# Two layers of a hybrid model on one core: where the two expert slots are added up

## The chip, the core and the metric

The kernel runs on one core of a Trainium2 chip. The metric is the device time of one execution in microseconds; the median of three runs of the kernel before is 1312.31 us (1311.45 to 1312.48). Shorter is better.

## The reference

The model takes x of shape (4, 256, 256) in float32, four sequences of 256 tokens with 256 features, and adds eight stages to it, each on a layer-normed copy. Stage 2 and stage 4 are the same expert stage, which the change touches; stage 3 is an attention over the 16 heads within a token. The others are two causal attentions, a gated delta rule and two dense feed-forward stages. The expert stage, shortened:

```
logits = x @ Wg.T                      # 8 experts
probs = softmax(logits)
rw, sel = top_k(probs, 2)
rw = rw / rw.sum(-1)                   # two gates per token
base1, base3 = x @ W1.T, x @ W3.T      # shared, F = 896
for k in range(2):                     # the two slots
    x1 = base1 + lora(A1, B1, sel[k])  # rank 32 per expert
    x3 = base3 + lora(A3, B3, sel[k])
    x2 = silu(x1) * x3                 # 896 per token
    down = x2 @ W2.T                   # shared weights
    a2 = (x2 @ A2.T)[sel[k]]           # 8 x 32, one expert's 32 kept
    out += (down + a2 @ B2[sel[k]]) * rw[k]
```

## The kernel before, in words

Everything stays in SBUF; weights are loaded once. A sequence is worked on alone, as two halves of 128 tokens, but the order of the work is written out by hand in `program` (line 423) so that stages of different sequences stand beside each other. Each engine runs the same `program` and executes its own table entry of each stage name, so the queue of every engine (TensorE, VectorE, ScalarE as ACT, GpSimd as POOL) follows the one written order. PSUM banks are handed out by a small planner, `Ring`, which takes the bank of the permitted lane that was claimed the longest ago.

An expert block is (k, s): layer part k (0 or 1) and sequence s (0 to 3), eight blocks. `experts` (line 590) loops over seven feature tiles m of 128 (F = 896) with a lag of two:

- `x_first` (k, (s, m)): eight 256-column float32 matmuls give x1 and x3 of tile m for slot 0 in one bank. ACT applies Silu (line 1329), VectorE multiplies (line 1725) into `x2T[s][:, 0, m]` and signals `x2_first`.
- `x_second`: four matmuls add to the same bank the difference between the adapters of slot 1 and slot 0; ACT and VectorE again, into `x2T[s][:, 1, m]`; the signal is the drain of the bank.
- `down` (line 909): for slot i and token half a, seven matmuls with `x2T[s][:, i, m]` as stationary operand and 512 moving columns, which are 256 of the shared down weights W2 and 256 of A2 for all experts. In four of the blocks (`weave`) slot 0's part is spread over the loop instead, as `down_sum` (line 922). VectorE then adds the first 256 columns times the gate to X (line 1740) and keeps the chosen expert's 32 of the other 256, times the gate (line 1744, with `onehotw`, built in `gates`, line 1690).
- `lora_t` and `lora` bring the adapters' second half.

`middle` (line 501) runs twice, for sequences (0, 1) and (2, 3). It weaves the block (0, b) with the attention within tokens (`token_heads`, line 570) of sequence a, and the block (1, a) with that of sequence b, where a is the first and b the second of the pair. That attention's products are 16 GpSimd operations of 128x1024 for a sequence (`head_prod`, line 2138), each reduced on VectorE (lines 1785 and 1803); a buffer holds four of them. At the end `head_out_t` transposes the result on TensorE, inside the down group of slot 1 (place "down10": behind the first token half). GpSimd has otherwise only the powers of the norms (line 2116) and some work of the delta rule. The block (0, a) has no head products beside it; neither has (1, b).

Of the kernel before, what the change touches and what calls it, by code (L numbers as in the profile page):

```python
# [12 lines left out]
P = 128  # L13
B, T, D = 4, 256, 256
S = 2
# [83 lines left out]
def hybrid_kernel(nc, x_in, masks, packs, where, out):  # L99
    with ExitStack() as ctx:  # L100
# [81 lines left out]
        for s in range(S):  # L182
            v, o = part(s, 0, [4, T]); aT.append(v)
            v, o = part(s, o, [2, 4, T]); amT.append(v)
            v, o = part(s, o, [SX, T]); silu_x.append(v)
            v, o = part(s, o, [2, FT, T]); x2T.append(v)
            v, _ = part(s, 0, [NT, ER]); am2.append(v)
            v, _ = part(s, NT * ER, [NT, ER]); am2b.append(v)
            v, _ = part(s, 4 * T, [KER, T]); am2T.append(v)
        lg = alternate(lambda s: sb(f"lg{s}", [P, NT, E]))  # L190
        top = alternate(lambda s: sb(f"top{s}", [P, NT, 8]))
        topi = alternate(lambda s: sb(f"topi{s}", [P, NT, 8], U32))
# [112 lines left out]
        top_exp = each("top_exp")  # L305
        onehot_ready = each("onehot_ready")
        am_ready = each("am_ready")
        silu_ready = each("silu_ready")
        x2_first = each("x2_first")
        am2_ready = each("am2_ready")  # L310
# [98 lines left out]

        halves, weave, summing, alone, scores_first = [False], [False], [False], [False], [False]  # L410

        def lanes(name, k, s):

            if weave[0]:
                late = range(6, 8) if summing[0] else range(4, 8)
                return dict(x_first=range(0, 4), down=range(0, 4), down_sum=range(4, 6)).get(name, late)
            if not halves[0]:
                return range(BANKS)
            if s % 2 == 0:
                return range(0, 3)  # L420
# [169 lines left out]
        def experts(stage, k, s, beside):  # L590

            def others(slot):
                for b in beside.get(slot, ()):
                    stage(*b)

            for m in range(FT + 2):
                if m < FT and (m or (k == 0 and s % 2 == 0)):
                    stage("x_first", k, (s, m))
                others(f"f{m}")
                if m >= 2:  # L600
                    stage("x_second", k, (s, m - 2))
# [80 lines left out]
        def _(pe):  # L682
# [186 lines left out]
            def spread(k, s):  # L869
# [3 lines left out]
                for i in range(2):  # L873
# [35 lines left out]
            def down(k, sia):  # L909
# [6 lines left out]
                for m in range(FT):  # L916
                    if i == 1 and a == 0:
                        wait_drained(pe, ("x", r, m))
                    last = mm(o[:, :], x2T[s][:, i, m, a * P:(a + 1) * P], wd[:, m, :], m == 0, m == FT - 1)
                last.then_inc(full[ring.bank(("down", r, i, a))], 1)  # L920

            def down_sum(k, sm):
# [3 lines left out]
                pe.wait_ge(x2_first[s], nth(s, 2 * FT, k * FT + m + 1))  # L926
                for a in range(NT):
                    o = claim(pe, ("down", r, 0, a)) if m == 0 else bank[ring.bank(("down", r, 0, a))]
                    last = mm(o[:, :], x2T[s][:, 0, m, a * P:(a + 1) * P], wd[:, m, :], m == 0, m == FT - 1)
# [281 lines left out]
            def ffn_half(k, sa):  # L1211
# [11 lines left out]
                if a == NT - 1 or r in LAST:  # L1223
                    last.then_inc(full[ring.bank(key)], 1)

            table = dict(head_prod=nothing, spread2=nothing, delta_sq=nothing, consts=nothing, top_exp=nothing, ffn_half=ffn_half, delta_expand=nothing, delta_diag=nothing, conv_tap=nothing, gates=nothing, down_sum=down_sum, angles=nothing, norm_x=nothing, norm_t=norm_t, latent=latent, kv=kv, kv_fold=kv_fold,
                         scores=scores, weights=weights, values=values, values_t=values_t, out_in=out_in, out_proj=out_proj, router=router, spread_t=spread_t, spread=spread, x_first=x_first,
                         x_second=x_second, down=down, lora_t=lora_t, lora=lora,
                         heads_in=heads_in, head_scores=nothing, head_mix=nothing, head_out_t=head_out_t,
# [16 lines left out]
        def _(act):  # L1246
# [70 lines left out]
            def silu(k, s, i, m):  # L1317
# [4 lines left out]
                if n >= SX:  # L1322
# [163 lines left out]
            def angles(_, s):  # L1486
# [7 lines left out]
            table = dict(head_prod=nothing, spread2=nothing, delta_sq=nothing, consts=nothing, top_exp=top_exp_, ffn_half=nothing, delta_expand=nothing, delta_diag=nothing, conv_tap=conv_tap, gates=nothing, down_sum=nothing, angles=angles, norm_x=nothing, norm_t=norm_t, latent=latent, kv=nothing, kv_fold=nothing,  # L1494
                         scores=scores, weights=weights, values=values, values_t=nothing, out_in=out_in, out_proj=nothing, router=router, spread_t=spread_t, spread=nothing, x_first=x_first,
                         x_second=x_second, down=nothing, lora_t=lora_t, lora=nothing,
                         heads_in=heads_in, head_scores=head_scores, head_mix=nothing, head_out_t=head_out_t,
# [14 lines left out]
        def _(dve):  # L1512
# [177 lines left out]
            def gates(k, s):  # L1690
# [43 lines left out]
            def down(k, sia):  # L1734
# [5 lines left out]
                link(dve.scalar_tensor_tensor(out=X[s][:, a, :], in0=o[:, 0, :],  # L1740
                                              scalar=rw[s][:, i, a:a + 1], in1=X[s][:, a, :],
                                              op0=ALU.mult, op1=ALU.add))
# [319 lines left out]
            def angles(_, s):  # L2062
# [15 lines left out]
                for i, (quarter, shift) in enumerate(((0.0, 0.0), (0.25, PI2 / 4))):  # L2078
# [11 lines left out]
                    if i == 0:  # L2090
                        plink(ins)
                ins.then_inc(trig_in, 1)

            table = dict(head_prod=nothing, spread2=spread2, delta_sq=delta_sq, consts=consts, top_exp=nothing, ffn_half=nothing, delta_expand=delta_expand, delta_diag=delta_diag, conv_tap=conv_tap, gates=gates, down_sum=nothing, angles=angles, norm_x=norm_x, norm_t=nothing, latent=latent, kv=kv, kv_fold=kv_fold,
                         scores=scores, weights=weights, values=values, values_t=values_t, out_in=nothing, out_proj=out_proj, router=router, spread_t=nothing, spread=spread, x_first=x_first,
                         x_second=x_second, down=down, lora_t=lora_t, lora=lora,
                         heads_in=heads_in, head_scores=head_scores, head_mix=head_mix, head_out_t=nothing,
# [13 lines left out]
        def _(pool):  # L2111
# [71 lines left out]
            def delta_o(_, s):  # L2183
# [4 lines left out]
            table = dict(head_prod=head_prod, spread2=nothing, delta_sq=delta_sq, consts=nothing, top_exp=nothing, ffn_half=nothing, delta_expand=nothing, delta_diag=nothing, conv_tap=nothing, gates=nothing, down_sum=nothing, angles=nothing, norm_x=norm_x, norm_t=nothing, latent=nothing, kv=nothing, kv_fold=nothing,  # L2188
                         scores=nothing, weights=nothing, values=nothing, values_t=nothing, out_in=nothing, out_proj=nothing, router=nothing, spread_t=nothing, spread=nothing, x_first=nothing,
                         x_second=nothing, down=nothing, lora_t=nothing, lora=nothing,  # L2190
                         heads_in=nothing, head_scores=nothing, head_mix=nothing, head_out_t=nothing,
                         head_out=nothing, delta_gate=delta_gate, delta_conv=nothing, delta_log=nothing, delta_g1=delta_g1, conv_silu=nothing,
                         delta_qk=nothing, delta_on=nothing,
# [118 lines left out]
```

## Time and profile before

| what | value |
|---|---|
| median of three runs | 1312.31 us |
| the profiled execution | 1312.18 us |
| its span | 1310.4 us |
| TensorE busy | 1202.5 us, 92% |
| VectorE busy | 677.2 us, 52% |
| ScalarE busy | 416.9 us, 32% |
| GpSimd busy | 229.6 us, 18% |
| mean granted TensorE clock | 0.983 of full speed |

The span is the time between the first and the last record of the profile; the execution's own time holds some 2 us more. A float32 matmul shows as two records. The durations of matmul records overlap, so the price of one is read from the distance between starts.

### The profile page before, as it was taken

To read this page: it belongs to the slowest core of one execution; us is meant where nothing else is said; L and a number is where in the kernel's file an instruction comes from. 1 tells how busy PE (TensorE), PEld (TensorE's weight loads), DVE (VectorE), ACT (ScalarE), POOL (GpSimd) and SP (SyncE) were. 2 spreads that over 40 slices of the span, in tenths; PEclk is the share of its full clock that TensorE was granted. 3 is DMA by queue.
4 is the path that set the end of the run, shared out by engine and by line. 5 is a ranking of instruction groups with operands and counts; after the bars stand their busy time and mean duration, and the time that the engine had idled before them with its cause. 6 is when DMAs were issued, how large, how long until landed. Compare 5 with 4: busy or idle time off the path is not lost.

```text
span 1310.4 us, 17604 instructions
## 1 busy us (share of the span) xinstructions
PE 1202.5 (92%) x6865; PEld 916.2 (70%) x6865; DVE 677.2 (52%) x1661; ACT 416.9 (32%) x897; POOL 229.6 (18%) x133
## 2 busy tenths in 40 slices
PE   6889999999998989988787999999999989899888
PEld 5677675767866778667565776757678677786666
DVE  5753266664465456334634433666644655663351
ACT  3623021313222342433453431313133223424352
POOL 0000074560110210000000000836501102100000
PEclk9999999999999999989998999999999999998989
DMA  8200000000000000000000000000000000000000
GB/s 350 115 1 1 1 1 1 1 1 1 1 1 2 1 1 1 1 2 9 1 9 1 1 1 1 1 0 1 0 1 1 1 1 1 1 1 2 1 1 17
DMA packets 3570, 17.32 MB, mean 13 GB/s; under 512 B 288, under 2 KB 2464, under 8 KB 2976
## 3 DMA queue, kind: packets, MB, share of 16 engines
q1 hardware_dynamic: 2912, 14.12, 2.7%
q10 hardware_dynamic: 576, 2.08, 0.4%
q8 instruction: 55, 0.90, 0.3%
q14 instruction: 27, 0.22, 0.1%
HBM read 15.15 MB, written 1.05 MB: 12 GB/s over the span
## 4 chain that ended last, share of the span: by engine, by line
PE 70%; DVE 11%; issue 9%; ACT 6%; POOL 2%; DMA 0%; DVEq 0%; POOLq 0%; ACTq 0%
PE bank L684 66%; ACT scr L1278 3%; PE bank L701 2%; DVE XnT L1960 2%; DVE XnT L1962 1%; DVE scr L1552 1%; DVE stat L1544 1%; POOL rstd L2116 1%; DVE negmax L1634 1%; PE bank L802 1%; DVE X L1537 1%; PE bank L1089 1%; ACT scr L1256 1%; POOL fac L2116 1%; ACT XnT L1256 1%
## 5 line engine op out<-in xcount | busy, mean ns | idle before, releaser
L684 PE MATMUL bank<-pack,scr 128*128 128x512 f32 (+2 forms) x944 | 312.1, 483 | 8.5 <-ACT scr L1256 7.5
L684 PE MATMUL bank<-XnT,pack 128*128 128x256 f32 x1024 | 251.3, 385 | 11.9 <-ACT XnT L1256 7.1
L684 PEld LDWEIGHTS bank<-pack,scr 128*128 128x128 f32 x944 | 178.5, 193 | 114.9 <-issue 89.4
L684 PE MATMUL bank<-scr,pack 128*128 128x256 f32 x944 | 227.0, 380 | 1.3 <-DVE scr L1715 1.1
L684 PEld LDWEIGHTS bank<-XnT,pack 128*128 128x128 f32 x1024 | 191.7, 192 | 45.4 <-ACT XnT L1256 9.6
L684 PEld LDWEIGHTS bank<-scr,pack 128*128 128x128 f32 x944 | 178.1, 190 | 30.3 <-issue 4.4
L2138 POOL TENSOR_TENSOR scr<-scr 128x1024 f32<-128x1024 f32 x64 | 149.9, 2379 | 47.3 <-DVEq L1777 46.6
L2116 POOL TENSOR_TENSOR rstd<-veps,half 128x2 f32<-128x2 f32 x32 | 22.3, 698 | 750.2 <-DVE veps L1549 750.2
L1725 DVE TENSOR_TENSOR scr<-bank,scr 128x256 f32<-128x256 f32 x112 | 47.2, 423 | 149.5 <-ACT scr L1329 148.6
L1278 ACT ACTIVATE scr<-bank,negmax 128x256 f32<-128x256 f32 (+1 forms) x256 | 82.9, 445 | 92.5 <-DVE negmax L1634 92.5
L1329 ACT ACTIVATE scr<-bank 128x256 f32<-128x256 f32 x112 | 42.6, 384 | 210.5 <-PE bank L684 210.3
L1256 ACT ACTIVATE scr<-bank 128x512 f32<-128x512 f32 (+7 forms) x112 | 51.0, 474 | 176.8 <-PE bank L701 90.0
L684 PE MATMUL bank<-scr 32*128 32x128 f32 (+4 forms) x944 | 78.8, 322 | 1.3 <-ACT scr L1256 1.3
L684 PEld LDWEIGHTS bank<-scr 32*128 32x128 f32 (+2 forms) x944 | 65.7, 186 | 19.8 <-issue 9.0
L1632 DVE TENSOR_REDUCE negmax<-bank 128x2 f32<-128x512 f32 x64 | 43.8, 684 | 68.0 <-PE bank L684 68.0
L1256 ACT ACTIVATE mats<-bank 128x512 f32<-128x512 f32 (+1 forms) x80 | 42.6, 555 | 106.4 <-PE bank L1089 83.7
L1537 DVE TENSOR_TENSOR X<-bank,X 128x512 f32<-128x512 f32 x31 | 21.4, 691 | 94.2 <-PE bank L684 94.2
L802 PE MATMUL bank<-pack,scr 128*128 128x128 f32 x384 | 55.6, 295 | 8.2 <-ACT scr L1278 7.6
L701 PE MATMUL bank<-pack,scr 128*128 128x128 f32 x232 | 38.0, 292 | 24.5 <-DVE scr L1552 15.6
L684 PE MATMUL bank<-identb 128*128 128x512 bf16 x197 | 55.6, 383 | 5.0 <-DVE scr L1656 3.9
L802 PEld LDWEIGHTS bank<-pack,scr 128*128 128x128 f32 x384 | 46.5, 151 | 14.9 <-ACT scr L1278 11.6
L701 PEld LDWEIGHTS bank<-pack,scr 128*128 128x128 f32 x232 | 28.7, 149 | 39.9 <-issue 20.3
(178 smaller groups left out, 1384.9 us busy)
## 6 DMA issues: line engine op xcount, KB each, us to landing
pack<-pack_dram SPq DMA_DIRECT2D x1, 6152.0 KB, 17.5
pack<-pack_dram SPq DMA_DIRECT2D x1, 2180.0 KB, 29.6
pack<-pack_dram SPq DMA_DIRECT2D x1, 1595.0 KB, 23.5
X<-x SPq DMA_DIRECT2D x4, 256.0 KB, 16.9
pack<-pack_dram SPq DMA_DIRECT2D x1, 1024.0 KB, 20.3
pack<-pack_dram ACTq DMA_DIRECT2D x1, 975.5 KB, 6.3
pack<-pack_dram SPq DMA_DIRECT2D x1, 793.5 KB, 25.0
out_dram<-X SPq DMA_DIRECT2D x3, 256.0 KB, 2.1
```

The lines of the kernel that those rows point to most:

```text
L684: return pe.matmul(o, l, r, start=start, stop=stop, skip_group_check=True)
L701: last = pe.transpose(o[:, t * T + a * P:t * T + a * P + P], src(t, a), ident)
L802: last = pe.transpose(o[:, (c - 4 * b) * P:(c - 4 * b + 1) * P], prob[s][:, u % PR, c * P:(c + 1) * P], ident)
L1256: act.activation(dst, src, func, **kw).then_inc(drain_of(key), 1)
L1278: ins = act.activation(prob[s][:, u % PR, j * HW + lo:j * HW + hi], psum(key, BANK)[:, lo:hi], ACT.Exp, bias=negmax[s][:, u % PR, tile, j: ...
L1329: act.activation(silu_x[s][:, n % SX, :], psum(key, T), ACT.Silu).then_inc(silu_ready[s], 1)
L1537: dve.tensor_tensor(xf, psum(key, n), xf, ALU.add).then_inc(drain_of(key), 1)
L1632: dve.tensor_reduce(negmax[s][:, u % PR, 1, 2 * h:2 * h + 2], o[:, :, P:HW], AX.X, ALU.max, negate=True).then_inc(max_ready[s], 1)
L1725: dve.tensor_tensor(x2T[s][:, i, m, :], psum(key, 2, T)[:, 1, :], silu_x[s][:, n % SX, :], ALU.mult)\
L1960: link(dve.tensor_tensor(t, rows16[:, 0:i + 1, :, i].rearrange("p j m -> p m j"), solved(s)[:, :, 0:i + 1], ALU.mult))
L2116: return pool.tensor_tensor(dst, src, half[:, 0:1].broadcast_to(shape) if len(shape) == 2 else half[:, 0:1].unsqueeze(1).broadcast_to(shap ...
L2138: pool.tensor_tensor(prod[s][:, hh], *pairs, ALU.mult).then_inc(hprod_ready[s], 1)
```

## The change

In six of the eight blocks, all but (1, 1) and (1, 3), the two slots are joined before the shared down weights. `joined` says which. With r = gate 1 / gate 0, down is computed as gate 0 * (x2 of slot 0 + r * x2 of slot 1) @ W2. GpSimd scales the second slot's tile by r and adds the first slot's, in place, tile by tile; r is needed along the features' layout (tokens along the free axis), so VectorE writes r of each token as a row of 128 columns, TensorE turns it with two 128x128 matmuls, and ACT moves the result to SBUF. The matmuls of slot 0 keep the 256 columns of A2 alone; those of slot 1 keep all 512. A2 of slot 1 is then applied to the sum, so `onehotw` holds for slot 0 the difference of the two one-hot rows times gate 0, and for slot 1 its one-hot row times gate 0. VectorE's addition to X is left out for slot 0.

```diff
+        def joined(k, s):
+            return k == 0 or s % 2 == 0
...
             for m in range(FT + 2):
+                if m == 0 and joined(k, s):
+                    stage("ratio_rows", k, s)
                 if m < FT and (m or (k == 0 and s % 2 == 0)):
                     stage("x_first", k, (s, m))
+                if m == 1 and joined(k, s):
+                    stage("ratio", k, s)
...
+            def ratio(k, s):                                   # TensorE
+                pe.wait_ge(ratio_ready[s], nth_sum(k, s, 1, 1))
+                o = claim(pe, ("ratio", (k, s)))
+                for a in range(NT):
+                    last = mm(o[:, a * P:(a + 1) * P], ratio_w[s][:, a, :], ident, True)
+                last.then_inc(full[ring.bank(("ratio", (k, s)))], 1)
...
                 for m in range(FT):                            # TensorE, down
                     if i == 1 and a == 0:
                         wait_drained(pe, ("x", r, m))
-                    last = mm(o[:, :], x2T[s][:, i, m, a * P:(a + 1) * P], wd[:, m, :], m == 0, m == FT - 1)
+                    if i == 1 and a == 0 and joined(k, s):
+                        pe.wait_ge(sum_ready[s], nth_sum(k, s, FT, m + 1))
+                    c0 = D if i == 0 and joined(k, s) else 0
+                    last = mm(o[:, c0:2 * D], x2T[s][:, i, m, a * P:(a + 1) * P], wd[:, m, c0:2 * D],
+                              m == 0, m == FT - 1)
...                                                            # the same columns in down_sum
+            def ratio(k, s):                                   # ACT
+                key = ("ratio", (k, s))
+                wait_full(act, key)
+                move(key, ratio_t[s], psum(key, T))
...
+                if joined(k, s):                               # VectorE, gates
+                    link(dve.tensor_tensor(onehotw[s][:, :, 0, :], onehot[s][:, :, 0, :], onehot[s][:, :, 1, :],
+                                           ALU.subtract))
+                    for a in range(NT):
+                        step(dve.tensor_scalar(onehotw[s][:, a, 0, :], onehotw[s][:, a, 0, :], rw[s][:, 0, a:a + 1],
+                                               None, ALU.mult))
+                        step(dve.tensor_scalar(onehotw[s][:, a, 1, :], onehot[s][:, a, 1, :], rw[s][:, 0, a:a + 1],
+                                               None, ALU.mult))
+                    settle()
+                    return
...
+            def ratio_rows(k, s):                              # VectorE
+                dve.wait_ge(top_exp[s], nth(s, 2, k + 1))
+                dve.tensor_copy(ratio_w[s], rw[s][:, 2, :].unsqueeze(2).broadcast_to([P, NT, P]))\
+                   .then_inc(ratio_ready[s], 1)
...
+                if i or not joined(k, s):                      # VectorE, down
+                    link(dve.scalar_tensor_tensor(out=X[s][:, a, :], in0=o[:, 0, :],
+                                                  scalar=rw[s][:, 0 if joined(k, s) else i, a:a + 1],
+                                                  in1=X[s][:, a, :], op0=ALU.mult, op1=ALU.add))
...
+            def x_second(k, sm):                               # GpSimd
+                s, m = sm
+                if not joined(k, s):
+                    return
+                if m == 0:
+                    wait_drained(pool, ("ratio", (k, s)))
+                pool.wait_ge(x2_first[s], nth(s, 2 * FT, k * FT + m + 1))
+                wait_drained(pool, ("x", (k, s), m))
+                x2 = x2T[s][:, 1, m, :]
+                pool.tensor_tensor(x2, x2, ratio_t[s], ALU.mult).then_inc(scaled[s], 1)
+                pool.wait_ge(scaled[s], nth_sum(k, s, FT, m + 1))
+                pool.tensor_tensor(x2, x2, x2T[s][:, 0, m, :], ALU.add).then_inc(sum_ready[s], 1)
```

## Rows read from the trace of the kernel before

**Rows 1.** Page, part 1: busy us (share of the span) and instructions of each engine.

```profile
PE 1202.5 (92%) x6865; PEld 916.2 (70%) x6865; DVE 677.2 (52%) x1661; ACT 416.9 (32%) x897; POOL 229.6 (18%) x133
```

**Rows 2.** Timeline of GpSimd: start us, length us, line, operation, count, idle before.

```profile
172.05 37.51 POOL L2138 TENSOR_TENSOR scr<-scr 128x1024 f32<-128x1024 f32 x16 [13.41 <-DVEq L1777]
...
244.34 28.05 POOL L2138 TENSOR_TENSOR scr<-scr 128x1024 f32<-128x1024 f32 x12 [9.84 <-DVEq L1777]
272.70 9.44 POOL L2138 TENSOR_TENSOR scr<-scr 128x1024 f32<-128x1024 f32 x4 [0.31 <-DVE scr L1803]
...
825.34 37.50 POOL L2138 TENSOR_TENSOR scr<-scr 128x1024 f32<-128x1024 f32 x16 [13.47 <-DVEq L1777]
```

**Rows 3.** Timeline of TensorE: down of the first block, and x_first in (0, 1).

```profile
123.93 24.20 PE L684 MATMUL bank<-pack,scr 128*128 128x512 f32 x56
...
155.63 1.03 PE L684 MATMUL bank<-XnT,pack 128*128 128x256 f32 x4
156.50 1.03 PE L684 MATMUL bank<-scr,pack 128*128 128x256 f32 x4
```

**Rows 4.** Timeline of TensorE: four records of 128x128 and the next row.

```profile
162.54 0.60 PE L701 MATMUL bank<-pack,scr 128*128 128x128 f32 x4
162.97 1.89 PE L684 MATMUL bank<-scr,pack 128*128 128x256 f32 x8
```

**Rows 5.** Timeline of VectorE and TensorE where (0, 1) begins its loop.

```profile
158.68 0.86 DVE L1552 TENSOR_SCALAR scr<-X,mv,rstd 128x256 f32<-128x256 f32 x2 [0.81 <-POOL rstd L2116]
159.09 1.03 PE L684 MATMUL bank<-XnT,pack 128*128 128x256 f32 x4
```

**Rows 6.** Groups by line and form, VectorE: count, busy us, mean ns, idle before.

```profile
L1790 DVE TENSOR_TENSOR scr<-scr,bmax 128x256 f32<-128x256 f32 x8 | 9.8, 1222 | 0.3
...
L1643 DVE COPY scr<-bank 128x256 f32<-128x256 f32 x12 | 5.0, 415 | 3.0 <-PE bank L684 3.0
```

**Rows 7.** Timeline of VectorE before the head products of (1, 0).

```profile
237.66 0.87 DVE L1698 TENSOR_SCALAR onehotw<-pack,topf,rw 128x8 f32<-128x8 f32 x4
238.98 0.88 DVE L1767 TENSOR_TENSOR scr<-bank,cos_t 128x256 f32<-128x256 f32 x2 [0.45 <-PE bank L684]
```

**Rows 8.** Timeline of VectorE and TensorE at the end of (0, 1).

```profile
208.41 0.41 DVE L1725 TENSOR_TENSOR scr<-bank,scr 128x256 f32<-128x256 f32 x1
...
211.11 0.42 DVE L1807 TENSOR_TENSOR scr<-scr,bmax 128x256 f32<-128x256 f32 x1
212.06 0.60 PE L701 MATMUL bank<-pack,scr 128*128 128x128 f32 x4
```

**Rows 9.** Timeline of TensorE at the end of (1, 0).

```profile
292.95 0.60 PE L701 MATMUL bank<-pack,scr 128*128 128x128 f32 x4
```

**Rows 10.** Groups by line and form, GpSimd.

```profile
L2138 POOL TENSOR_TENSOR scr<-scr 128x1024 f32<-128x1024 f32 x64 | 149.9, 2379 | 47.3 <-DVEq L1777 46.6 <-DVE scr L1803 0.6
...
L2157 POOL TENSOR_TENSOR mats<-pack,small 128x768 f32<-128x768 f32 x8 | 11.6, 1472 | 37.5 <-DVE small L1879 37.5
...
L2176 POOL TENSOR_TENSOR scr<-scr,small 128x384 f32<-128x384 f32 x8 | 6.5, 831 | 0.0
```

**Rows 11.** Timeline of VectorE: the last product of slot 1 in (0, 0).

```profile
124.55 0.42 DVE L1725 TENSOR_TENSOR scr<-bank,scr 128x256 f32<-128x256 f32 x1 [0.57 <-ACT scr L1329]
```

**Rows 12.** Timeline of TensorE and VectorE in down of (0, 2).

```profile
768.79 7.91 PE L684 MATMUL bank<-pack,scr 128*128 128x256 f32 x22
773.57 0.86 DVE L1552 TENSOR_SCALAR scr<-X,mv,rstd 128x256 f32<-128x256 f32 x2 [0.81 <-POOL rstd L2116]
776.53 0.60 PE L701 MATMUL bank<-pack,scr 128*128 128x128 f32 x4
```

**Rows 13.** Stretches: start:end, us, TensorE busy (records), granted clock, DMA share, GB/s.

```profile
649.20:652.90 3.70, 0.09 (x5) 1.00 0.00 0
653.00:656.20 3.20, 3.20 (x16) 0.50 0.02 5
```

More of the change, by code:

```diff
@@ L189, in hybrid_kernel @@
             v, _ = part(s, 4 * T, [KER, T]); am2T.append(v)
+        ratio_t = alternate(lambda s: aT[s][:, 2, :])
+        ratio_w = alternate(lambda s: aT[s][:, 3, :].rearrange("p (a t) -> p a t", a=NT))
         lg = alternate(lambda s: sb(f"lg{s}", [P, NT, E]))
@@ L307, in hybrid_kernel @@
         am_ready = each("am_ready")
+        ratio_ready = each("ratio_ready")
+        scaled = each("scaled")
+        sum_ready = each("sum_ready")
         silu_ready = each("silu_ready")
@@ L410, in hybrid_kernel, with nth_sum @@
         halves, weave, summing, alone, scores_first = [False], [False], [False], [False], [False]
+        def joined(k, s):
+            return k == 0 or s % 2 == 0
+        JOINED = [[k for k in range(2) if joined(k, s)] for s in range(S)]
+        def nth_sum(k, s, per, n):
+            ks = JOINED[s % S]
+            return nth(s, per * len(ks), ks.index(k) * per + n)
         def lanes(name, k, s):
@@ L419, in lanes @@
             if s % 2 == 0:
-                return range(0, 3)
+                return range(3, 8) if name == "ratio" else range(0, 3)
             return dict(values=range(3, 4), scores=range(4, 8), weights=range(4, 8)).get(name, range(3, 8))
@@ L928, in down_sum @@
                     o = claim(pe, ("down", r, 0, a)) if m == 0 else bank[ring.bank(("down", r, 0, a))]
-                    last = mm(o[:, :], x2T[s][:, 0, m, a * P:(a + 1) * P], wd[:, m, :], m == 0, m == FT - 1)
+                    c0 = D if joined(k, s) else 0
+                    last = mm(o[:, c0:2 * D], x2T[s][:, 0, m, a * P:(a + 1) * P], wd[:, m, c0:2 * D],
+                              m == 0, m == FT - 1)
                     if m == FT - 1:
@@ L1224, in ffn_half @@
                     last.then_inc(full[ring.bank(key)], 1)
-            table = dict(head_prod=nothing, spread2=nothing, delta_sq=nothing, consts=nothing, top_exp=nothing, ffn_half=ffn_half, delta_expand=nothing, delta_diag=nothing, conv_tap=nothing, gates=nothing, down_sum=down_sum, angles=nothing, norm_x=nothing, norm_t=norm_t, latent=latent, kv=kv, kv_fold=kv_fold,
+            table = dict(ratio=ratio, ratio_rows=nothing, head_prod=nothing, spread2=nothing, delta_sq=nothing, consts=nothing, top_exp=nothing, ffn_half=ffn_half, delta_expand=nothing, delta_diag=nothing, conv_tap=nothing, gates=nothing, down_sum=down_sum, angles=nothing, norm_x=nothing, norm_t=norm_t, latent=latent, kv=kv, kv_fold=kv_fold,
                          scores=scores, weights=weights, values=values, values_t=values_t, out_in=out_in, out_proj=out_proj, router=router, spread_t=spread_t, spread=spread, x_first=x_first,
@@ L1492, in angles @@
                 act.activation(expA[:, :], w("c_alog"), ACT.Exp).then_inc(trig_out, 1)
-            table = dict(head_prod=nothing, spread2=nothing, delta_sq=nothing, consts=nothing, top_exp=top_exp_, ffn_half=nothing, delta_expand=nothing, delta_diag=nothing, conv_tap=conv_tap, gates=nothing, down_sum=nothing, angles=angles, norm_x=nothing, norm_t=norm_t, latent=latent, kv=nothing, kv_fold=nothing,
+            table = dict(ratio=ratio, ratio_rows=nothing, head_prod=nothing, spread2=nothing, delta_sq=nothing, consts=nothing, top_exp=top_exp_, ffn_half=nothing, delta_expand=nothing, delta_diag=nothing, conv_tap=conv_tap, gates=nothing, down_sum=nothing, angles=angles, norm_x=nothing, norm_t=norm_t, latent=latent, kv=nothing, kv_fold=nothing,
                          scores=scores, weights=weights, values=values, values_t=nothing, out_in=out_in, out_proj=nothing, router=router, spread_t=spread_t, spread=nothing, x_first=x_first,
@@ L2092, in angles @@
                 ins.then_inc(trig_in, 1)
-            table = dict(head_prod=nothing, spread2=spread2, delta_sq=delta_sq, consts=consts, top_exp=nothing, ffn_half=nothing, delta_expand=delta_expand, delta_diag=delta_diag, conv_tap=conv_tap, gates=gates, down_sum=nothing, angles=angles, norm_x=norm_x, norm_t=nothing, latent=latent, kv=kv, kv_fold=kv_fold,
+            table = dict(ratio=nothing, ratio_rows=ratio_rows, head_prod=nothing, spread2=spread2, delta_sq=delta_sq, consts=consts, top_exp=nothing, ffn_half=nothing, delta_expand=delta_expand, delta_diag=delta_diag, conv_tap=conv_tap, gates=gates, down_sum=nothing, angles=angles, norm_x=norm_x, norm_t=nothing, latent=latent, kv=kv, kv_fold=kv_fold,
                          scores=scores, weights=weights, values=values, values_t=values_t, out_in=nothing, out_proj=out_proj, router=router, spread_t=nothing, spread=spread, x_first=x_first,
@@ L2186, in delta_o @@
                       [P, NT * GH]).then_inc(orms[s], 1)
-            table = dict(head_prod=head_prod, spread2=nothing, delta_sq=delta_sq, consts=nothing, top_exp=nothing, ffn_half=nothing, delta_expand=nothing, delta_diag=nothing, conv_tap=nothing, gates=nothing, down_sum=nothing, angles=nothing, norm_x=norm_x, norm_t=nothing, latent=nothing, kv=nothing, kv_fold=nothing,
+            table = dict(ratio=nothing, ratio_rows=nothing, head_prod=head_prod, spread2=nothing, delta_sq=delta_sq, consts=nothing, top_exp=nothing, ffn_half=nothing, delta_expand=nothing, delta_diag=nothing, conv_tap=nothing, gates=nothing, down_sum=nothing, angles=nothing, norm_x=norm_x, norm_t=nothing, latent=nothing, kv=nothing, kv_fold=nothing,
                          scores=nothing, weights=nothing, values=nothing, values_t=nothing, out_in=nothing, out_proj=nothing, router=nothing, spread_t=nothing, spread=nothing, x_first=nothing,
-                         x_second=nothing, down=nothing, lora_t=nothing, lora=nothing,
+                         x_second=x_second, down=nothing, lora_t=nothing, lora=nothing,
                          heads_in=nothing, head_scores=nothing, head_mix=nothing, head_out_t=nothing,
```

3 lines of the change are left out of this document (removed).

## The prediction

> **What bounds the kernel now.** I read the page first: TensorE is busy for 92% of the span, GpSimd for 18% [rows 1]. By that average the change takes work from the full engine and gives it to an empty one. The average is the wrong view, so I went to GpSimd's timeline. Of its 229.6 us, 149.9 are the 64 head products, in four bursts of 16. Each burst is one unbroken run of about 37.5 us: 172.05 to 209.56, 244.34 to 282.14 (with one break of 0.3), and the same two again in the second half of the kernel, from 825.34 on [rows 2]. The bursts lie inside four of the six expert blocks that are changed: in each half of the kernel the block (k=0, second sequence), here A, and (k=1, first sequence), here B. The other two changed blocks, (0, first sequence) of each half, have no head products beside them.
>
> Then I looked at where A ends. TensorE's last down group runs to 212.06, and the transposes of the head context come right behind it [rows 8]. They need the last reduction and scaling on VectorE (211.11 + 0.42), which follows the last head product by 2 us. So TensorE's and GpSimd's chains end A within half a microsecond of each other. In B the same place is at 292.95 [rows 9], while GpSimd is through at 282.14: some 10 us of room.
>
> **What TensorE saves.** Each changed block has 14 matmuls of slot 0 (7 tiles, 2 token halves) that go from 512 to 256 columns. Fifty-six records, 28 matmuls at 512 columns, take 24.2 us from 123.93 on: 0.86 each. At 256 columns four records (two matmuls) go every 0.865 us, 0.43 each [rows 3]. So 14 x 0.43 = 6.0 us a block, 36 in all. The two added 128x128 matmuls that spread the ratio have the form of the transposes: four records in 0.43 us [rows 4]. VectorE loses two L1740 a block and gains one copy of 128x256 (about 0.42, [rows 6]) and two small operations in the gates; ACT gains one 0.4 us move. Neither engine sets the pace there.
>
> **A small new wait on TensorE.** The ratio matmuls stand behind x_first of tile 1, and their rows come from VectorE behind the norm. In A that norm ends at 159.54, so the copy ends near 159.96, where TensorE now starts x_first of tile 2 at 159.09 [rows 5]: 0.9 us of waiting and 0.43 of work, 1.3 us, which heads_in and the first head product inherit. In the first block I take 0.3 + 0.43 for the same. In B VectorE gains 0.5 us of gates and the copy, less the 0.45 for which it sat idle before heads_in [rows 7]: the first head product is 0.5 us later.
>
> **What GpSimd gets.** Fourteen operations of 128x256 with two SBUF inputs a block: for each of seven tiles a multiply, a wait on its own semaphore, an add. The trace has no such operation. From below: a quarter of the 128x1024 pitch (37.51/16 = 2.34), 0.59 us. From above: the 128x384 operation, 0.83. The step from 384 to 768 elements costs 0.64 us, which leaves a fixed 0.19 [rows 10]; with the fixed part under the 1024 operation, whose inputs are both read in full as these are, 256 elements cost 0.19 + 2.15/4 = 0.73, with the slope of the 384 and 768 ones 0.62. I take 0.70, 1.44 us for a pair p with its wait (bounds 1.2 and 1.7).
>
> The Trainium skill ("GPSIMD Engine Reference", section 3.1) gives 4497 ns for such an operation on 2048 elements, and 4.1 advises VectorE for elementwise work. With this trace's 2.34 for 1024 the figure makes an estimate of 0.73 us at 256, p about 1.5, and the sum below 1.6 us higher. No run here shows the 2048 figure.
>
> **Block A.** GpSimd works in program order, and down of slot 1, first half, now waits tile by tile for the sums. The order is: pair 0 (before the heads are ready, free), products 0 to 4, pair 1, 5 and 6, pair 2, 7 to 9, pair 3, 10 to 12, pair 4, 13 to 15, pairs 5 and 6. No pair waits for VectorE: the last slot-1 product stood at 208.41 [rows 8], ahead of its turn, and it remains so. From 172.05 + 1.3 = 173.4, 37.5 us of head products and 6p = 8.6 lead to 219.5; one 512-column matmul and the semaphore, 0.9, make 220.4, where the transposes stood at 212.06: **+8.4 us**. TensorE by itself would have come there at 212.06 + 1.3 - 6.0 = 207.4, so all of its saving turns into waiting, between about 205 and 219.5. Even with p = 0 the head products alone would hold it until 211.8. What follows (head_out, norm, second half of down) is unchanged and shifts whole.
>
> **Block B.** From 244.8, 37.5 and 7p = 10.1 lead to 292.4 and with the 0.9 to 293.3, against 292.95: **+0.4 us**. TensorE itself would be there at 287.4, so the 10 us of room and the saving are both used up.
>
> **The two blocks without heads.** In the first, the last slot-1 product ends at 124.97 [rows 11]; its pair is through by 126.5, and slot 0's fourteen matmuls last until 130.0. So there is no stall: -6.0 + 0.4 + 0.3 = **-5.3**. In the second half's one, the first seven matmuls cover a norm: its output is ready at 774.43, and TensorE, now there at 776.53, would come 3.0 earlier, at 773.5 [rows 12]. That stall gives back 1.0: -6.0 + 0.4 + 1.0 = **-4.6**.
>
> **Sum without the clock:** -5.3 - 4.6 + 2 x 8.4 + 2 x 0.4 = +7.7 us. Written in p it is -29.9 + 26p: zero at p = 1.15, an operation of 0.55.
>
> **The clock.** After TensorE did 0.09 us of work in 3.7, the granted clock was 0.50 in the 3.2 us that followed, the 1.2 GHz level instead of 2.4 [rows 13]. In A TensorE has gaps of about 5 and 8 us just before the stretch that is then critical, in B one of about 4. A stretch of 3.2 us at half clock loses 1.6 us where TensorE is the path. I take 1.6 to 1.7 in A and 0.9 in B (part of it falls into waits), 5 us in all; bounds 0 and 8. The Trainium skill ("TensorE: Matmul & The Clock Gate", "What's actually happening") says that an idle TensorE falls back to half clock; the trace agrees, and without that rule the time would be 5 us lower.
>
> The forecast: 7.7 + 5 = 12.7 us on the profiled execution's 1312.18 (span 1310.4), which lies 0.1 under the median: **1325 us**.
>
> **Rivals.**
> 1. The forecast's mechanism with low prices: p = 1.2 and a clock that stays up. -29.9 + 31.2 = +1.3: **1313.6**, no change. For it: only these rows bound p, and the clock may catch the gap late. Against: it needs a quarter of the large operation, without the fixed part that 384 and 768 show.
> 2. Faster. GpSimd's small operations cost 0.45 us or less, p = 0.95 (below my lower bound): -29.9 + 24.7 = -5.2 and no clock loss, **1307**. It decides from p = 1.15 down. For it: the measured gaps between GpSimd's operations are nil, and spans on GpSimd are rough. Against: the pitch of the head products is no rough span, it is 16 of them in 37.5 us.
> 3. The saving comes through whole, because the pairs slip into time that GpSimd has: 36 - 2.6 of ratio matmuls - 3 of waits leaves **1282**. The page's 18% speaks for it. The unbroken bursts speak against it, and in A the head products alone exclude it.
> 4. Slower still: p = 1.7, as for 384 elements, and 8 us of clock: -29.9 + 44.2 + 8 = +22.3, **1334.5**. VectorE operations with two SBUF inputs that meet GpSimd's would push this way: inside the bursts L1790, 256 elements, takes 1.22 us in the mean [rows 6].
>
> **Chances.** Forecast 0.70, its own range 1316 to 1333; rival 1 0.10; rival 2 0.07; rival 3 0.03; rival 4 0.10. About 0.2%, 2.6 us, is what a measurement here can tell from no change. Rival 1 falls inside it, mostly, and some of rival 2: faster 0.09, same 0.08, slower 0.83. The range is 1311 to 1334: rival 1 in, the faster ones and part of rival 4 out.
>
> **What would show it.** In the changed kernel: the matmuls of slot 0 at 256 columns, 0.43 apart; GpSimd's operations on 128x256 near 0.7; bursts of GpSimd without a break of some 46 us; TensorE idle before the last matmuls of down slot 1 in A, some 12 us with a release by GpSimd, and about 4 to 6 in B; a granted clock of 0.5 behind them; 4.5 to 5.3 us saved in each block without heads. I am wrong if the bursts have gaps, if VectorE does not come late with the head reductions, or if operations of GpSimd fall under 0.55.

## The result, and the profile after

The changed kernel takes 1328.9 us in the median of four runs (1327.48 to 1330.4), the kernel before, in the four runs beside it, 1312.39: a ratio of 1.0126, 95% interval 1.0109 to 1.0144. It is slower by 16.5 us; 12.7 were forecast, and the time lies inside the range. The profiled execution took 1327.48 us, its span is 1325.3.

Page of the changed kernel, part 1: busy us (share) and instructions.

```profile
PE 1184.6 (89%) x6889; PEld 921.9 (70%) x6889; DVE 676.9 (51%) x1661; ACT 418.2 (32%) x903; POOL 289.7 (22%) x217
```

Against [rows 1] TensorE does less and idles more: 18 us less busy in a span 15 us longer. Half clock hides part of what was saved, as a matmul at 1.2 GHz counts as busy for twice as long. GpSimd has 60.1 us more, for 84 operations. Groups by line and form, GpSimd (count, busy us, mean ns, idle before):

```profile
L2205 POOL TENSOR_TENSOR scr<-scr 128x1024 f32<-128x1024 f32 x64 | 148.8, 2357 | 29.0 <-DVEq L1831 29.0
L2186 POOL TENSOR_TENSOR scr<-scr 128x256 f32<-128x256 f32 x42 | 32.7, 778 | 107.5 <-DVE scr L1778 107.5
L2188 POOL TENSOR_TENSOR scr<-scr 128x256 f32<-128x256 f32 x42 | 30.5, 726 | 3.3
```

The add takes 0.73 us, the multiply 0.78 in the mean. The head products are what they were in [rows 10]. Now GpSimd's timeline in A (start, length, count):

```profile
167.66 11.57 POOL L2205 TENSOR_TENSOR scr<-scr 128x1024 f32<-128x1024 f32 x5 [4.62 <-DVEq L1831]
179.16 0.94 POOL L2186 TENSOR_TENSOR scr<-scr 128x256 f32<-128x256 f32 x1
180.18 0.72 POOL L2188 TENSOR_TENSOR scr<-scr 128x256 f32<-128x256 f32 x1
180.86 4.64 POOL L2205 TENSOR_TENSOR scr<-scr 128x1024 f32<-128x1024 f32 x2
...
204.06 6.90 POOL L2205 TENSOR_TENSOR scr<-scr 128x1024 f32<-128x1024 f32 x3
210.90 0.74 POOL L2186 TENSOR_TENSOR scr<-scr 128x256 f32<-128x256 f32 x1
211.72 0.72 POOL L2188 TENSOR_TENSOR scr<-scr 128x256 f32<-128x256 f32 x1
212.40 0.91 POOL L2186 TENSOR_TENSOR scr<-scr 128x256 f32<-128x256 f32 x1
213.38 0.72 POOL L2188 TENSOR_TENSOR scr<-scr 128x256 f32<-128x256 f32 x1
```

The burst that ran from 172.05 for 37.51 us [rows 2] now runs from 167.66 to 214.10, 46.4 us, with no idle time named on any row after the first. VectorE is not what A waits for: its last scaling of the head context (L1861) ends at 212.72, 3.4 us ahead of the transposes.

```profile
212.24 0.48 DVE L1861 TENSOR_TENSOR scr<-scr,bmax 128x256 f32<-128x256 f32 x1
```

TensorE's timeline at the end of A answers to [rows 8]:

```profile
196.36 4.46 PE L704 MATMUL bank<-pack,scr 128*128 128x256 f32 x12
204.25 2.05 PE L704 MATMUL bank<-pack,scr 128*128 128x512 f32 x2 [3.43 <-POOL scr L2188]
212.58 3.75 PE L704 MATMUL bank<-pack,scr 128*128 128x512 f32 x4 [6.29 <-POOL scr L2188]
216.13 1.06 PE L721 MATMUL bank<-pack,scr 128*128 128x128 f32 x4
```

The last sums that TensorE waits for come from GpSimd's add (L2188), 3.43 and then 6.29 us late. The two last matmuls take 3.55 us from start to the next row, where two took 1.72 before. The granted clock in the same places, in A and then in B (start:end, us; busy of TensorE, weight loads, VectorE, ScalarE, GpSimd; then the granted clock, the DMA share and GB/s):

```profile
204.20:212.50 8.30, 2.05 (x2) 0.50 (x2) 5.09 (x6) 0.00 (x0) 8.22 (x6) 0.50 0.00 0
212.60:216.10 3.50, 3.50 (x4) 1.23 (x5) 0.88 (x3) 0.00 (x0) 1.43 (x2) 0.50 0.00 0
289.40:293.80 4.40, 0.14 (x1) 0.00 (x0) 3.06 (x4) 0.00 (x0) 4.32 (x5) 0.85 0.00 0
293.85:299.10 5.25, 5.25 (x6) 1.86 (x7) 1.23 (x4) 0.00 (x0) 2.85 (x4) 0.50 0.00 0
```

In B TensorE, after a wait of 4.32 us for the fifth of the seven sums, does the last three matmuls of this down group at half clock; the transposes stand at 299.10, against 292.95 [rows 9].

A good ruler for the whole kernel is the power of each layer norm on GpSimd (line 2116 before, 2170 after): 32 marks in both traces, in the same order. The offset of a mark is its start less the start before, in us:

```
mark (start before)                    after   e1     e2     e3     e5     e6     e7     e4
before the first block, 87.07          -1.05  -0.45  -0.37  -0.90  -0.08  -0.02   0.10  -0.74
behind (0, 0), 157.94                  -5.66  -5.06  -5.39  -5.51  -0.07  -4.63  -4.50  -5.37
behind A, 217.52                        4.53  -5.06   0.16   3.37  10.14  -4.63  -4.50  -5.37
behind B, 298.41                        6.28  -5.06  -4.06   3.89  10.14  -4.14   8.76  -5.37
behind the delta rule, 700.15           8.17  -0.65  -7.63   1.55  10.12  -3.65   7.00  -1.29
before down of (0, 2), 772.84           8.63  -0.25  -7.13   2.00  10.12  -3.12   7.49  -0.87
behind (0, 2), 811.18                   3.72  -5.16 -12.04  -2.91  10.11  -8.03   2.58  -5.78
behind the second A, 870.74            13.89  -5.15  -5.73   6.06  19.77  -8.01   2.59  -5.77
behind the second B, 951.63            15.49  -5.15  -9.84   6.60  19.77  -6.46  15.93  -5.77
last mark, 1290.61                     14.86  -8.62 -12.20   5.58  16.29  -6.85  13.31   1.36
```

The column "after" is the whole result: 4.6 gained in the block (0, 0), 10.2 lost in A, 1.75 in B; in the second half 4.45 gained, 10.2 and 1.6 lost. The stages in between, which the change does not touch, shift by +1.9 us in "after" over the stretch 314.69 to 700.15, and by -3.6 to +4.4 in the other columns (e4 left out, which joins a block there). Half clock falls on them in other places each time; cut into slices of 4 us, the stretch 404 to 520 has two below 0.97 in the trace before (at 452 and 456) and five in the one after (448, 452, 460, 464, 480). Added up over 314.69 to 700.15 from the granted clock in slices of 1 us, TensorE stands at half clock for some 20 us before, 27 after, 38 in e1, 17 in e2, 14 in e3. The shifts go the same way (+1.9, +4.4, -3.6, -2.3); only e7, with 20 us and -1.9, does not fit.

One of the four runs of e5 below took 1584.4 us at a mean granted clock of 0.743 and is left out of its numbers.

### The profile page after: what moved, and what is told of

Its sections match the earlier page's. It is cut to its first block, busy times and chain, and to the rows that moved or that the text cites. A ratio compares the mean times of both kernels' runs of the same rounds, so it can differ in the third digit from the quotient of the medians.

```text
span 1325.3 us, 17828 instructions
## 1 busy us (share of the span) xinstructions
PE 1184.6 (89%) x6889; PEld 921.9 (70%) x6889; DVE 676.9 (51%) x1661; ACT 418.2 (32%) x903; POOL 289.7 (22%) x217
## 4 chain that ended last, share of the span: by engine, by line
PE 56%; DVE 16%; issue 10%; POOL 10%; ACT 7%; DMA 0%; DVEq 0%; POOLq 0%; ACTq 0%
PE bank L704 52%; POOL scr L2205 6%; ACT scr L1311 3%; PE bank L721 2%; DVE XnT L2014 2%; DVE XnT L2016 1%; DVE scr L1590 1%; DVE stat L1582 1%; POOL rstd L2170 1%; DVE scr L1839 1%; DVE X L1575 1%; DVE negmax L1672 1%; PE bank L822 1%; DVE scr L1857 1%; POOL scr L2186 1%
## 5 line engine op out<-in xcount | busy, mean ns | idle before, releaser
L704 PE MATMUL bank<-pack,scr 128*128 128x256 f32 (+3 forms) x968 | 290.0, 451 | 38.6 <-POOL scr L2188 28.2
L704 PEld LDWEIGHTS bank<-pack,scr 128*128 128x128 f32 x968 | 182.1, 195 | 125.4 <-issue 93.1
L704 PE MATMUL bank<-XnT,pack 128*128 128x256 f32 x1024 | 255.8, 390 | 12.3 <-ACT XnT L1289 7.1
L721 PEld LDWEIGHTS bank<-pack,scr 128*128 128x128 f32 x232 | 29.2, 151 | 41.2 <-issue 22.7
L2186 POOL TENSOR_TENSOR scr<-scr 128x256 f32<-128x256 f32 x42 | 32.7, 778 | 107.5 <-DVE scr L1778 107.5
```

The costliest lines, as they stand in the source:

```text
L704: return pe.matmul(o, l, r, start=start, stop=stop, skip_group_check=True)
L721: last = pe.transpose(o[:, t * T + a * P:t * T + a * P + P], src(t, a), ident)
L2186: pool.tensor_tensor(x2, x2, ratio_t[s], ALU.mult).then_inc(scaled[s], 1)
```

## The experiments

The median of the kernel before was 1312.8 us beside the first four and 1314.6 beside the last three (with runs from 1308.0 to 1322.5), where the expectations start from 1312.4. The ratios are those on record, with their 95% intervals; they differ a little from the quotients of the medians (0.9912 for e1, 1.0084 for e7). What one block costs is read from the marks.

**Only the blocks without heads (e1).**

```diff
-            return k == 0 or s % 2 == 0
+            return k == 0 and s % 2 == 0
```

> The slots are joined only in the two blocks (0, first sequence of each half), which have no head products beside them. Theory (GpSimd's unbroken bursts set the ends of the woven blocks, the joining itself is sound): only the two gains of the prediction are left, 5.3 + 4.6, in the trace of the changed kernel 5.7 + 4.9, so 1302 us (1300 to 1304), with no stretch of half clock near 205 or 870. Rival (the ratio's copy, matmuls and moved banks cost more than the halved columns give, and the woven blocks only add to it): 1311 or more. Rival (a saving of TensorE's is given back later by the delta rule's waits): 1306 to 1312.

1301.3 us, ratio 0.9891 (0.9861 to 0.9921). Faster by 1.1%, as expected. Column e1 has -4.6 in (0, 0), nothing in A and B, -4.9 across down of (0, 2). It is the best of all versions here, and the trace has no half clock in A or B. Both rivals are out by their own numbers. But in the profiled execution the stages behind do take back most of the first gain: the offset rises from -5.1 to -0.7 in the delta rule between, where half clock grew from some 20 to 38 us, and the -5.16 later on is the second block's gain, not the first one's come back. The -8.6 at the end holds another -3.5 of the tail, where half clock shrank from some 20 to 3 us. The blocks alone are worth 4.6 + 4.5 = 9.1 us; the medians differ by 11.5, and for the other 2.4 there is no trace.

**A pair of one operation (e2).** The multiply by the ratio is left out, so the second slot is summed unscaled.

```diff
-                pool.tensor_tensor(x2, x2, ratio_t[s], ALU.mult).then_inc(scaled[s], 1)
-                pool.wait_ge(scaled[s], nth_sum(k, s, FT, m + 1))
```

> As the changed kernel, but GpSimd's multiply by the ratio is left out with its wait (the second slot is added unscaled), so a pair of 1.49 us is one operation of some 0.75. Theory (the ends of A and B stand at burst + 6 pairs and burst + 7 pairs): A comes 6 x 0.74 = 4.4 us earlier, B 7 x 0.74 = 5.2, together 19 us, and B's clock loss goes: 1328.9 - 19 - 2 = 1308 us (1304 to 1311). Rival (TensorE's end in A and B is set by VectorE, or by the order of banks, and GpSimd is only near): 1322 or more. The multiply is doubled by nothing else, so any value between tells the share of GpSimd's.

1306.0 us, ratio 0.9955 (0.9912 to 0.9998); the first theory's. The first A costs 5.55 us instead of 10.19, so 4.6 less for six multiplies of 0.78 (4.7); the second costs 6.31 instead of 10.17, only 3.9 less. So in the first A the time follows GpSimd's operations one for one. B goes from a loss of 1.75 to a gain of 4.22, and in the second half from 1.60 to a gain of 4.11. Without the 1.2 and 1.1 us of half clock that also go (e3 below) that is 4.7 and 4.6, where seven multiplies are 5.5: GpSimd's last operation waits 1.09 us for VectorE's product there, so GpSimd alone no longer holds the end of B. In A TensorE still waits 6.44 us for GpSimd, and the last two matmuls still run at half clock for the most part (3.30 us from start to the next row, against 1.72; granted clock 0.54). The transposes behind them are at full clock again (0.60). In the second A half clock lasts through the transposes too (3.55 us and 1.06), which makes some 0.7 us of the difference between the two. TensorE in the first A, and GpSimd's last operation in B:

```profile
201.38 1.10 PE L704 MATMUL bank<-pack,scr 128*128 128x512 f32 x2 [1.83 <-POOL scr L2186]
208.91 3.46 PE L704 MATMUL bank<-pack,scr 128*128 128x512 f32 x4 [6.44 <-POOL scr L2186]
212.21 0.60 PE L721 MATMUL bank<-pack,scr 128*128 128x128 f32 x4
```

```profile
287.09 0.72 POOL L2186 TENSOR_TENSOR scr<-scr 128x256 f32<-128x256 f32 x1 [1.09 <-DVE scr L1778]
```

**TensorE kept busy while it waits (e3).**

```diff
                 o = claim(pe, ("down", r, i, a))
+                if i == 1 and a == 0 and weave[0] and joined(k, s):
+                    warm(o, 54 if k == 0 else 27)
```

> As the changed kernel, with 54 (A) and 27 (B) bf16 matmuls of 512 columns into the bank that the first token half of down slot 1 has just claimed, ahead of it, so that TensorE does not idle before the stretch that waits for GpSimd. Theory (the clock term is real: the stretch behind GpSimd runs at 0.50): the granted clock stays at 1.00 there, A gains 1.5 to 2 us, B 1 to 1.5, and the time falls to 1322 us (1319 to 1325). Rival (half clock falls into waits and costs nothing, the whole loss is GpSimd's): 1328 to 1330, with the ends of A and B where they were.

`warm(o, n)` issues n dummy matmuls into the bank, whose content the down matmuls then replace. 1317.7 us, ratio 1.0040 (1.0012 to 1.0068): faster than the changed kernel, and 1.3 us below the range. The rival is out. The stretches hold the clock (TensorE in A, then all engines in A and B):

```profile
197.37 11.82 PE L704 MATMUL bank<-identb 128*128 128x512 bf16 x54
209.03 5.31 PE L704 MATMUL bank<-pack,scr 128*128 128x512 f32 x12
214.49 1.10 PE L704 MATMUL bank<-pack,scr 128*128 128x512 f32 x2 [0.15 <-POOL scr L2190]
215.43 0.60 PE L721 MATMUL bank<-pack,scr 128*128 128x128 f32 x4
```

```profile
197.40:215.40 18.00, 17.85 (x69) 7.89 (x68) 11.74 (x15) 0.00 (x0) 16.71 (x12) 1.00 0.01 1
284.80:296.80 12.00, 12.00 (x42) 5.25 (x41) 5.90 (x9) 0.00 (x0) 10.72 (x9) 1.00 0.00 0
```

A costs 8.88 and 8.97 instead of 10.19 and 10.17, B 0.52 and 0.54 instead of 1.75 and 1.60. That is 1.3 and 1.2 in A, 1.2 and 1.1 in B, 4.8 us for the clock in the four blocks, less in each of them than was expected. In B the seven matmuls follow the dummies without a wait (290.61 to 296.83), within 0.2 us of where GpSimd's last sum would let them end. The medians differ by 11.2 us, so the time fell by more than this mechanism gives. Some 4.6 of the other 6.4 are the untouched stages of these two profiled executions (the delta rule and its surroundings -2.3 against +1.9, the tail -1.0 against -0.6); half clock takes some 14 us of the stretch 314.69 to 700.15 instead of 27. Whether the dummy matmuls bring that about, or the clock merely fell elsewhere, these runs do not tell.

**The other blocks without heads as well (e4).** Joined in (0, first) and (1, second); in the latter the ratio's matmuls stand ahead of x_first of tile 1.

```diff
-            return k == 0 or s % 2 == 0
+            return (k == 0) == (s % 2 == 0)
...
+                if k == 1 and m == 1 and joined(k, s):
+                    stage("ratio", k, s)
                 if m < FT and (m or (k == 0 and s % 2 == 0)):
                     stage("x_first", k, (s, m))
-                if m == 1 and joined(k, s):
+                if k == 0 and m == 1 and joined(k, s):
                     stage("ratio", k, s)
```

> The slots are joined in the four blocks that have no head products beside them: (0, first) and also (1, second) of each half; in the latter the ratio's matmuls stand ahead of the second tile. Theory (TensorE bound wherever GpSimd has room): the two of the first run gain their 10, the new two less than 5.6 each, because their first seven matmuls of slot 0 end 0.7 us before a wait for VectorE (L1901) already: 1 to 3 each, 1298 us (1295 to 1301). Rival (GpSimd's large powers of the delta rule, 4.2 us, now stand behind the sums and delay the rule): 1302 or more, no better than the run with two blocks.

1316.9 us, ratio 1.0038 (1.0022 to 1.0054): missed by 19 us. The time is in the rival's range. Where column e4 stands at -5.4 behind B and the first power of the delta rule (363.12 before) is due next, it stands at +3.85: the joined block (1, 1) loses 9.2 us. TensorE's timeline has the cause:

```profile
314.40 1.22 PE L706 MATMUL bank<-pack,scr 128*128 128x128 f32 x4 [4.10 <-DVE scr L1754]
315.42 1.91 PE L706 MATMUL bank<-XnT,pack 128*128 128x256 f32 x4
317.12 1.91 PE L706 MATMUL bank<-scr,pack 128*128 128x256 f32 x4
318.83 1.87 PE L706 MATMUL bank<-XnT,pack 128*128 128x256 f32 x4
...
374.45 0.33 PE L1073 MATMUL bank<-pack,scr 128*128 128x128 f32 x1 [3.94 <-DVE scr L1957]
```

The ratio's rows (L1754) come late, as VectorE has the norm and the masks before them: 4.10 us of waiting. Then four records of 256 columns take 1.7 us instead of 0.865, until 320.54. The two make 7.8 us by 328.77. And the wait for L1957 has grown from 0.71 to 3.94, which takes up what the narrower matmuls of slot 0 save. It hangs on GpSimd's power at 366.97, 0.1 us behind the last sum:

```profile
366.14 0.72 POOL L2190 TENSOR_TENSOR scr<-scr 128x256 f32<-128x256 f32 x1
366.97 4.16 POOL L2172 TENSOR_TENSOR fac<-ss,half 128x24 f32<-128x24 f32 x1
```

The rival's mechanism, sums that delay this power, is not what the rows show: VectorE's input to it (L1946) ends only at 366.90, itself 3.9 us later than before, and GpSimd is free at 366.86. Of these 3.9, at most some 0.2 are GpSimd's: L1946 takes 0.41 us beside the last sum instead of 0.18. The power is late because the block lost its time at the start. I had counted what stood around `down`, not where the new wait begins. How much the joining would bring here with the ratio in a better place stays open; no later place was run.

**A alone (e5).**

```diff
-            return k == 0 or s % 2 == 0
+            return k == 0 and s % 2 == 1
```

> The slots are joined only in A, the block (0, second sequence) of each half. Theory (each woven block ends by its own GpSimd burst, independent of the others): A costs what the offsets in the changed kernel's trace say, 10.2 us each, 8.9 of them GpSimd's length and 1.3 the clock, so 1312.4 + 20.4 = 1333 us (1330 to 1336). Rival (A's loss in the changed kernel comes from being reached 5.7 us earlier, with the head products unable to start earlier): then A alone, reached at the old time, costs less, 5 or so each, 1323.

1329.8 us (three runs, 1328.5 to 1332.9), ratio 1.0121 (1.0092 to 1.0149), 0.2 us below the range. A costs 10.2 and 9.7 us also where nothing ahead of it is faster. The rival, a loss from arriving early, is out. The sum was 20.4 us and the ratio gives 16: in the profiled execution the two blocks lose 19.9 and the tail gives 3.5 back, with half clock down from some 20 to 3 us there.

**B on GpSimd (e6).** `joined` returns `s % 2 == 0`.

> The slots are joined in the blocks without heads of the first sequences and in B, (1, first sequence); GpSimd does the sums in both. Theory: the two gains of 5.1 stay, B costs 1.7 each with its clock loss: 1312.4 - 10.2 + 3.4 = 1305.6 us (1303 to 1309), so worse by 3 to 4 than the kernel that joins the two blocks without heads alone. Rival (B pays once A does not delay it): 1298 or less.

1305.4 us, ratio 0.9946 (0.9927 to 0.9965), as expected. B costs 0.5 and 1.6 us, with a mean granted clock of 0.64 and 0.51 over the last three matmuls of the down group; 1.7 each were expected. With e1's two gains kept, joining B adds work and brings nothing.

**B on VectorE (e7).** As e6, but with k = 1 the pair stands in VectorE's queue:

```diff
             def x_second(k, sm):                               # VectorE
                 product(k, sm[0], 1, sm[1])
+                s, m = sm
+                if not joined(k, s) or k == 0:
+                    return
+                if m == 0:
+                    wait_drained(dve, ("ratio", (k, s)))
+                wait_drained(dve, ("x", (k, s), m))
+                x2 = x2T[s][:, 1, m, :]
+                dve.tensor_tensor(x2, x2, ratio_t[s], ALU.mult).then_inc(scaled[s], 1)
+                dve.wait_ge(scaled[s], nth_sum(k, s, FT, m + 1))
+                dve.tensor_tensor(x2, x2, x2T[s][:, 0, m, :], ALU.add).then_inc(sum_ready[s], 1)
...
             def x_second(k, sm):                               # GpSimd
                 s, m = sm
-                if not joined(k, s):
+                if not joined(k, s) or k == 1:
```

> As the run with GpSimd in B, but in B VectorE does the multiply and the add. Theory (only the place of the work is wrong; but VectorE operations with two SBUF inputs wait for the end of GpSimd's running head product, as L1790 does at 1.22 us against 0.42): 14 operations of 1.2 us are 17 us in B, where VectorE has 12.8 us free and TensorE ends 5.6 sooner, so B ends 3 to 8 us later than before: 1312.4 - 10.2 + 2 x 5 = 1312 us (1307 to 1318), and the rows show these operations far above 0.42. Rival (no waiting between the two engines, 0.42 each, 6 us in free time): B gains its 5.6, 1297 to 1300, the best of all.

1325.6 us, ratio 1.0069 (1.0041 to 1.0096): missed, 7.6 us above the range. B costs 13.3 us both times, more than my 3 to 8; the rival, no waiting, is out. VectorE's rows:

```profile
L1793 DVE TENSOR_TENSOR scr<-scr 128x256 f32<-128x256 f32 x14 | 18.4, 1313 | 0.6
L1795 DVE TENSOR_TENSOR scr<-scr 128x256 f32<-128x256 f32 x14 | 14.0, 1002 | 0.5
...
L1854 DVE TENSOR_TENSOR scr<-scr,bmax 128x256 f32<-128x256 f32 x8 | 12.1, 1508 | 0.3
```

```profile
engine op xcount: duration ns min/median/max, first and last start us, forms
L1793 DVE TENSOR_TENSOR scr<-scr x14: 424/1536/2328, 247.8 to 957.0; 128x256 f32<-128x256 f32 x14
```

Alone, the multiply takes 0.42 us; beside head products up to 2.33, the length of one. Seven pairs are 16.2 us, near the 17 expected. What I had left out is the way back: VectorE's reductions come late, the buffer of four products stays full, and GpSimd, whose burst had no gap, now waits:

```profile
261.34 7.13 POOL L2215 TENSOR_TENSOR scr<-scr 128x1024 f32<-128x1024 f32 x3 [2.53 <-DVE scr L1849]
269.97 2.33 POOL L2215 TENSOR_TENSOR scr<-scr 128x1024 f32<-128x1024 f32 x1 [1.49 <-DVE scr L1849]
277.13 2.33 POOL L2215 TENSOR_TENSOR scr<-scr 128x1024 f32<-128x1024 f32 x1 [4.83 <-DVE scr L1867]
281.41 7.11 POOL L2215 TENSOR_TENSOR scr<-scr 128x1024 f32<-128x1024 f32 x3 [1.95 <-DVE scr L1867]
```

The Trainium skill says it in "SBUF — State Buffer", "SBUF: two separate sides": a VectorE operation with two SBUF inputs and a GpSimd operation that reads SBUF exclude each other for the whole instruction. The rows agree; the products of VectorE that read PSUM and SBUF keep their 0.42 us.

## Why the prediction was right

| step | forecast, us | measured, us | shown by |
|---|---|---|---|
| GpSimd pair p | 1.44 (1.2 to 1.7) | 1.49 | the burst in A, 46.44 less 37.5, over six |
| (0, 0) | -5.3 | -4.6 | offsets, e1 |
| (0, 2) | -4.6 | -4.45 | offsets, e1 |
| A without the clock, each | +8.4 | +8.9, +9.0 | e3 |
| B without the clock, each | +0.4 | +0.5, +0.5 | e3 |
| clock, A and B, all four | 5 | 4.8 | after less e3 |
| untouched stages | 0 | +0.2 | offsets |
| outside the marks | 0 | +0.4 | 15.3 less the last mark's 14.86 |
| sum on the profiled execution | +12.7 | +15.3 | 1327.48 less 1312.18 |

**The mechanism** stood as forecast. A ends by GpSimd's one queue: the burst plus six pairs. e2 takes half of each pair away and moves the first A by just that (the second by 0.8 less, most of it the clock's); e5 shows that A's loss needs no other block. Rival 3, the full saving, is excluded by A, and rivals 1 and 2 by the price: p is 1.49, well above 1.15, where the sum turns. Rival 4, p = 1.7 and 8 us of clock, is too dear in both terms. The idle time in A is near the 12 us of the signs: TensorE waits from 200.8 to 212.6 for sums, with one matmul in between (3.43 and 6.29 us). VectorE's head reductions come late, as the signs wanted: the last scaling ends at 212.72, 1.2 us later than before in a block begun 5.7 us earlier.

**The price of a small operation.** I had 0.70 from a fixed part and the slope of the 1024-element operation, and the measured 0.73 of the add is on the upper one of my two lines, the multiply's 0.78 above it. The estimate from the Trainium skill ("GPSIMD Engine Reference", 3.1) gave 0.73 and was the better. The multiply has 0.72 in most places and about 0.91 in others; I did not look for the cause. In the first A three of the six have 0.90 to 0.94, some 0.6 us in all, and a pair there goes every 1.50 or 1.70 us, 1.59 in the mean; the 16 head products take 36.9 us instead of 37.5, which is why the burst grows by only 1.49 a pair.

**The wait for the ratio** in A was forecast as 0.9 and is 0.56 at 154.14, the copy being faster (0.29 in place of 0.42), and the first head product starts 1.3 us later against the mark ahead of it, as said. In (0, 0) the wait is 0.83, in place of 0.74 there before for the norm, and one more of 0.45 appears at 104.17, where TensorE waits for a product of VectorE to clear a bank. I had not seen it; it is most of what that block falls short. In (0, 2) the wait before the transposes is 0.88, forecast 1.0:

```profile
777.42 4.92 PE L704 MATMUL bank<-pack,scr 128*128 128x256 f32 x22
783.22 0.63 PE L721 MATMUL bank<-pack,scr 128*128 128x128 f32 x4 [0.88 <-DVE scr L1590]
```

**B.** Forecast +0.4 and measured +0.5 at full clock: the ten microseconds of room and the 5.6 saved are both gone. The first head product there is 4.50 us later than before, and the mark ahead of it 4.53: the half microsecond I gave to the gates did not come. The gates have one more operation, where I had counted two, and those on 8 elements take 0.23 in place of 0.29.

**The clock** was right in sum and wrong in its parts: 1.6 to 1.7 in A and 0.9 in B were forecast, 1.3 and 1.2 in A and 1.2 and 1.1 in B measured. That the sum is so near is luck, as one error covers the other. In A the half clock begins near 204, over 8 us before the last two matmuls, and most of it falls into the wait.

**What is left over.** The blocks alone give +14.65, two above my 12.7: 0.7 in (0, 0), 0.15 in (0, 2), 0.3 in A, 0.75 in B. In A, 0.5 and 0.6 too little for GpSimd stand against 0.4 too much for the clock. The median lies another 1.4 above the profiled run, since two of the four runs are at 1330. What these two did otherwise has no trace.

## What to carry to other kernels

An engine that is idle for 82% of the span can be the bound of the very stage to which work is given. Look for its unbroken bursts on the timeline, and compare the end of each with the point where the chain needs it: the room there (0 in A, 10 us in B, the whole block in the others) decides, and it decided three ways in one change. So give such work out block by block: here the two blocks without head products are worth 1.1%, and the four with them turn that into a loss of 1.3%.

## What the runs showed of the hardware

- A GpSimd operation on two SBUF operands of 128x256 float32 takes 0.73 us as an add and 0.78 as a multiply in the mean (single multiplies 0.72 to 0.95), against 2.34 for 128x1024: a quarter of the elements at a third of the time.
- A VectorE operation on two SBUF operands of 128x256 takes 0.42 us, and up to 2.33 beside GpSimd's 128x1024 operations; its length then is up to that of one of them (e7).
- Behind waits of 3.4 to 6.4 us TensorE's granted clock was 0.50 to 0.64, that is mostly the 1.2 GHz level, also where a single matmul stood in the wait (204.25 in A). Dummy matmuls in the wait kept 2.4 GHz and were worth 1.1 to 1.3 us a time.
- The untouched stages between marks at 314.69 and 700.15 differ by up to 8.0 us from one kernel to another (+4.4 in e1, -3.6 in e2), mostly with the time at half clock (some 38 and 17 us there). A change of some 4 us is to be read from the block's own marks, and not from the median.
